# A top-k attention kernel: sums ahead of scores, the output copy behind the exponentials, key sums on GpSimd

## The reference

```python
q, k, v = split((xn @ Wqkv.T + bqkv))            # 16 heads of 8 channels, 256 rows
q, k = layernorm(q), layernorm(k)                # over the 8 channels
aw = softmax(q @ k.T / sqrt(8))                  # 256 x 256 for each head
aws = aw * (aw >= 12th largest of the row)       # top 5%
o_s = (aws / (sum(aws) + 1e-8)) @ v
qf, kf = softmax(q), softmax(k)                  # over the 8 channels
o_l = (qf @ (kf.T @ v)) / (qf . sum_rows(kf) + 1e-6)
o = sigmoid(alpha) * o_s + (1 - sigmoid(alpha)) * o_l
y = x + o @ Wproj.T + bproj + (xn @ W[idx] + b[idx])
```

## Time and profile before

| | before |
|---|---|
| median of three runs | 1290.69 us (1289.84 to 1293.82) |
| profiled execution | 1291.26 us, span of its instructions 1289.5 us |
| PE busy | 985.1 us, 76% |
| DVE busy | 1203.7 us, 93% |
| ACT busy | 1099.0 us, 85% |
| POOL busy | 1024.9 us, 79% |

### The profile page before, as it was taken

How to read it: one execution, slowest core, us unless ns; L and a number is a source line. 1 busy time by engine, 2 the same in 40 slices (tenths; PEclk the granted TensorE clock), 3 DMA queues, 4 the chain that set the end, 5 groups by cost and what they waited for, 6 DMA issues and landing times.

```text
span 1289.5 us, 38488 instructions
## 1 busy us (share of the span) xinstructions
PE 985.1 (76%) x9028; PEld 663.3 (51%) x9028; DVE 1203.7 (93%) x4585; ACT 1099.0 (85%) x3658; POOL 1024.9 (79%) x1560
## 2 busy tenths in 40 slices
PE   2578878888787777787877787777778788878876
PEld 0355555555455554555545555555545555555554
DVE  7699999999899998989989999999999999999994
ACT  2598989989899888979979989889988889989885
POOL 4587888988788887878968888888887888888864
PEclk9999999989899998989989999899999999999999
DMA  2122221212221222221222221222221222221120
GB/s 59 45 71 75 79 77 45 63 55 80 81 80 37 69 60 77 79 68 46 68 60 79 79 75 39 57 71 80 79 80 33 63 67 79 79 79 52 48 59 14
DMA packets 165203, 83.36 MB, mean 65 GB/s; under 512 B 7753, under 2 KB 164943, under 8 KB 164946
## 3 DMA queue, kind: packets, MB, share of 16 engines
q1 hardware_dynamic: 164946, 80.56, 21.7%
HBM read 42.78 MB, written 37.75 MB: 62 GB/s over the span
## 4 chain that ended last, share of the span: by engine, by line
DVE 31%; issue 24%; PE 18%; ACT 15%; POOL 6%; DVEq 4%; DMA 1%; SPq 0%; ACTq 0%; POOLq 0%
DVE rest L531 12%; DVE top L524 11%; ACT e L720 9%; DVE next L537 4%; POOL below L389 4%; PE turn_ps L831 4%; DVEq L73 3%; PE pv_ps L863 2%; ACT kept L685 2%; PE pv_ps L905 2%; PE turn_ps L832 2%; PE pv_ps L902 2%; PE work_ps L948 1%; ACT part L754 1%; PE score_ps L814 1%
## 5 line engine op out<-in xcount | busy, mean ns | idle before, releaser
L389 POOL TENSOR_SCALAR below<-e,next 128x256 bf16<-128x256 f32 x768 | 698.1, 928 | 0.0
L720 ACT ACTIVATE e<-score_ps,drop 128x256 f32<-128x256 f32 x1024 | 475.4, 490 | 68.1 <-POOL drop L367 67.2
L831 PE MATMUL turn_ps<-ident,e 128*128 128x128 f32 x2048 | 411.7, 294 | 28.1 <-issue 20.3
L531 DVE MATCH_REPLACE8 rest<-e 128x256 f32<-128x256 f32 x1024 | 413.8, 407 | 0.3
L537 DVE MAX8 next<-rest 128x8 f32<-128x256 f32 x1024 | 410.6, 411 | 0.8
L832 PE MATMUL turn_ps<-minus_huge,below 128*128 128x128 bf16 x2048 | 390.0, 228 | 0.0
L524 DVE MAX8 top<-score_ps 128x8 f32<-128x256 f32 x1024 | 360.0, 413 | 26.7 <-issue 15.0
L831 PEld LDWEIGHTS turn_ps<-ident,e 128*128 128x128 f32 x2048 | 303.8, 148 | 85.7 <-issue 42.5
L685 ACT ACTIVATE kept<-turn_ps 128x1024 f32<-128x1024 f32 x256 | 270.1, 1055 | 41.1 <-PE turn_ps L832 40.5
L720 ACT ACTIVATION_READ_ACCUMULATOR e<-score_ps,drop 128x1 f32 x1024 | 226.2, 221 | 0.0
L832 PEld LDWEIGHTS turn_ps<-minus_huge,below 128*128 128x128 bf16 x2048 | 225.7, 110 | 0.3 <-issue 0.2
(11 more groups left out here) (154 smaller groups left out, 1345.5 us busy)
## 6 DMA issues: line engine op xcount, KB each, us to landing
part_slots<-part SPq DMA_DIRECT2D x128, 192.0 KB, 2.3
q_slots<-part_slots SPq DMA_DIRECT2D x64, 256.0 KB, 3.5
k_slots<-part_slots SPq DMA_DIRECT2D x64, 256.0 KB, 4.1
part_slots<-part SPq DMA_DIRECT2D x64, 128.0 KB, 1.9
x_sb<-in_L_attn_x SPq DMA_DIRECT2D x32, 128.0 KB, 3.8
x_res<-in_L_attn_x SPq DMA_DIRECT2D x32, 128.0 KB, 4.0
out_y<-out_sb SPq DMA_DIRECT2D x32, 128.0 KB, 4.2
w_ops<-in_L_ffn_W SPq DMA_DIRECT2D x1, 512.0 KB
```

The source lines that it names most:

```text
L389: nc.gpsimd.tensor_scalar(below[:, r, t, :], e[:, r, t, :], next8[:, r, t, TOPK - 9:TOPK - 8], None, ALU.is_lt).then_inc(s["below_pool"], 1)
L531: nc.vector.match_replace(rest[:, t, :], e8[:, (u_ - 1) % 2, t, :], e[:, (u_ - 1) % RING, t, :], REMOVED).then_inc(s["rest_ready"], 1)
L720: nc.scalar.activation(e[:, u_ % RING, t, :], score_ps[:, u_ % 2, t // 2, t % 2, :], ACT.Exp, bias=drop[:, u_ % 2, t, 0:1], accum_out=z[:, ...
L831: mm(dst, e[:, r, t, keys], ident[:], start=True, stop=False, is_transpose=True)
```

## The change

Three edits:

1. On TensorE `sums()` of the sixth unit is called ahead of `early` and the scores, no longer behind the scores.
2. On GpSimd three additions (8 columns to 4 to 2 to 1, on 32 groups) make `k_sum` behind the comparisons of the sixth unit; VectorE's reduction goes. The reciprocal and the product stay, and wait for the same semaphore as before.
3. On ScalarE the copy to `out_sb` in the fourth unit stands behind that unit's exponentials and comparison, no longer ahead of them.

```diff
@@ tensors and semaphores
+        k_half = sb("k_half", [P, NT * H, 4])
+        k_quarter = sb("k_quarter", [P, NT * H, 2])
-            dmax_ready dsub_ready dexp_ready ksum_ready krec_ready feat_ready
+            dmax_ready dsub_ready dexp_ready ksum_step ksum_ready krec_ready feat_ready
@@ GpSimd
+                    if u_ == 5 and exists(it + 1):
+
+                        pool.wait_ge(s["dexp_ready"], 2 * (it + 2))
+                        src = k_exp[:].rearrange("p t (h d) -> p (t h) d", d=D)
+                        for i, (dst, w) in enumerate(((k_half[:], 4), (k_quarter[:], 2),
+                                                      (k_sum[:].unsqueeze(2), 1))):
+                            if i:
+                                pool.wait_ge(s["ksum_step"], 2 * (it + 1) + i)
+                            nc.gpsimd.tensor_tensor(dst, src[:, :, 0:w], src[:, :, w:2 * w], ALU.add).then_inc(
+                                s["ksum_step" if i < 2 else "ksum_ready"], 1)
+                            src = dst
@@ VectorE
-                    if u_ == 5 and exists(it + 1):
-                        if k == 5:
-
-                            dve.wait_ge(s["dexp_ready"], 2 * (it + 2))
-                            nc.vector.tensor_reduce(k_sum[:], k_exp[:].rearrange("p t (h d) -> p (t h) d", d=D), AX_X,
-                                                    ALU.add).then_inc(s["ksum_ready"], 1)
@@ ScalarE, ahead of the exponentials
-                    if u_ == 3 and exists(it - 2):
-                        act.wait_ge(s["w_out"], it - 1)
-                        wait(act, s["y_stored"], 16 * (it - 2))
-                        nc.scalar.copy(out_sb[:], pv_ps[:, 0:NT * C].rearrange("p (t c) -> p t c", t=NT)).then_inc(
-                            s["y_ready"], 1)
@@ ScalarE, behind the exponentials of keys and queries
+                    if u_ == 3 and exists(it - 2):
+                        act.wait_ge(s["w_out"], it - 1)
+                        wait(act, s["y_stored"], 16 * (it - 2))
+                        nc.scalar.copy(out_sb[:], pv_ps[:, 0:NT * C].rearrange("p (t c) -> p t c", t=NT)).then_inc(
+                            s["y_ready"], 1)
@@ TensorE
+                    if u_ == 5 and exists(it - 1):
+                        sums()
                     early(u_)
                     if exists(it if u_ < UNITS - 1 else it + 1):
                         scores(u_)
-                    if u_ == 5 and exists(it - 1):
-                        sums()
                     late(u_)
```

## The result

| | before | after |
|---|---|---|
| median, runs taken together on one chip | 1290.26 us (1289.61 to 1293.82) | 1255.66 us (1254.20 to 1259.08) |
| profiled execution, span | 1291.26, 1289.5 us | 1259.08, 1257.4 us |
| granted clock, mean | 0.958 | 0.967 |

The ratio is 0.973, 95% interval 0.9703 to 0.9757: 34.6 us less by the medians. The profiled execution of the kernel after is the slowest of its four, and its span is 32.1 us shorter than that of before; what follows explains these 32.1 us.

A forecast was written before the change was run, and what follows sets the result against it. VectorE, 93% busy, plus one wait per batch was taken as the bound. Gains of 28.0 + 9.9 us, less 2 and 3, took the profiled 1291.26 to 1258.4, so 1258 us; range 1251 to 1267, eight in ten 1250 to 1273.

The forecast's parts named there:

- VectorE's path is its work plus one wait: A normal batch, 37.75 us, is VectorE's work plus its 0.91 us wait for the sums' transposes; savings shorten the run.
- Term of the sums: Sixth unit, TensorE: transposes ahead of the scores remove VectorE's wait in 30 batches, 28.0 us gained.
- Term of the tree: VectorE loses the key sums' reduction, 0.32 us between starts, 31 times: 9.9 us gained.
- GpSimd's additions: Behind the sixth unit's thresholds, three additions take 1.1 us, covered by 1.47 us of idle time left on GpSimd.
- VectorE held by GpSimd: VectorE's replacements come 0.06 us later beside each tree of additions on GpSimd, 31 times: 2 us lost.
- The output copy: Fourth unit, ScalarE: the copy behind the exponentials frees 1.4 us that is slack, not gain: 0 us.
- Jumps and half clock: Behind the five loop jumps VectorE waits for TensorE at half clock, so part of the gain is lost: 3 us.
- rival 1: The earlier VectorE meets other late work in a batch's first units, giving back 16 us: 1274 us, chance 0.12.
- The rival of TensorE's clock: Half-clock stretches come into most batches, 3 us each; with 21 such batches 1321 us, chance 0.06.
- The wait stays: The sums' transposes still wait for ScalarE's later copy of oT, so VectorE waits as before: 1283 us, chance 0.05.
- VectorE stands still: VectorE stands for the whole 1.1 us of GpSimd's additions, 34 us in all: 1290 us, chance 0.03.

The follow-up runs named there:

- 1 + 3: Kernel before with the sums ahead of the scores and the output copy moved, VectorE's reduction kept: 1265.67 us, ratio 0.9798.
- 1: Kernel before with only the sums' transposes moved ahead of the remainder matmul and the scores: 1268.44 us, ratio 0.9832.
- 1 + 2: Kernel before with the sums ahead and the key sums added on GpSimd, output copy in its old place: 1262.02 us, ratio 0.9774.

## Why the prediction was right, and where it was not

The forecast was 1258 us, and 1255.66 came. The mechanism was right for the two terms that make the gain; that the number is so near is in part luck, as the sum below shows.

- *VectorE's path is its work plus one wait*: shown for the normal batch, which fell from 37.76 to 36.34 us, and by each of the first two edits by itself about as worked out. The prediction's list of waits left out a third, 11.3 us for scores in 10 places, and it is one of those that grew.
- *Term of the sums, 28.0 us*: per batch 0.99 us had been counted, 1.09 came. What was missed is that the step behind the wait is slower in the loop: 0.22 us from the denominators to the next maxima when VectorE had waited, 0.10 when not.
- *Term of the tree, 9.9 us, by the spacing of starts*: right in size in normal batches (0.32 to 0.36 us) and between "1 + 3" and the whole (10 us), but 6.4 us between "1" and "1 + 2" and 0.4 alone. The prediction added the terms without asking what each is worth alone. Why the other batches give it back without the sums is only in part shown, by the longer batches at the jumps.
- *GpSimd's additions, 1.1 us in a reserve of 1.47*: 1.14 us measured; 0.27 us of waiting is left, 0.37 by the forecast.
- *VectorE held by GpSimd, -2 us*: wrong, no run shows any. The 0.13 us of the earlier trace rows was read as a hold by the tree. Such a step occurs in 6 of 1024 pairs of the profile before, all six beside a squares' tree, but at one place of the loop, once in each of its six rounds; 24 other loads stand beside the same tree with the ordinary 0.06 us. The three other kernels that keep VectorE's reduction have six as well, the ten without it none, though all have the squares' tree, and the doubled tree has none beside it. So the odd step goes with the place in VectorE's code; what makes it is open. The rule of the Trainium skill (page "Perfetto Trace Analysis", section "Optimizing Scalar/DVE Operations"), that moving work between the two may not help since they share a port, did not decide here: for these instructions, with one tensor read each on VectorE's side, no run shows a hold.
- *The output copy, 0 us*: the size was off. It is worth 3 us alone, 3 with the sums (1268.44 - 1265.67) and about 6 with both others, the last just short of clear, and none of it in normal batches of the changed kernel. Why it matters is open; one profile of each is little, and written out the effect can't be told from nothing.
- *Jumps and half clock, -3 us*: mis-sized. The extra over normal batches grew by 8.5 us. Of that 6.2 are in the five batches with a jump: they got 0.18 us shorter each, where the other 24 got 1.33 us shorter. The prediction let some 0.5 us of the gain through there, and it counted only the waits for scores; the standing at the jump itself grew too, from 15.0 to 17.8 us in all. The other 2.3 us are mostly small waits for scores in batches without a jump: a part of rival 1 came true within the forecast.

The sum by what was measured: 29 batches of 1.42 us are 41.2 us, less 8.5 us of extra, is 32.7, and the profiled spans differ by 32.1. The forecast had 37.9, less 2 and 3. What it missed on the side of the gain (3.3 us, and 2 for a hold that isn't there) and on the side of the loss (5.5 us) cancelled: that is luck. The rival of TensorE's clock did not come: its mean rose from 0.958 to 0.967. "The wait stays" and "VectorE stands still" are refuted by the profile after.

## What to carry to other kernels

When one engine goes through a batch without a pause but for one wait, take its batch from one instruction to its next occurrence: work, by the distance between starts, plus that wait plus the slower step behind it. Ask of each edit what it is worth alone and behind the others: the same 0.3 us of every normal batch were worth 0.4, 6 and 10 us. Compare the normal batch and the rest apart: here the first followed the arithmetic to 0.1 us, while the second, with jumps back and half clock, held 29.8 us, and writing the loop out of the changed kernel was worth three quarters of the whole change.

## What the runs showed of the hardware

- A jump back of a loop of four batches leaves VectorE standing for 2.7 to 4.7 us (2.7 to 3.5 before, 3.1 to 3.7 after, 3.9 to 4.7 with smaller first loads), and TensorE's granted clock is 0.50, which is 1.2 of 2.4 GHz, in the stretch behind (483.6 to 493.8 us above). Five jumps and what followed cost 25.5 us (1255.66 - 1230.12).
- Behind a wait the step from the denominators to the next maxima is 0.22 us in the loop and 0.12 in the written-out batches, and 0.10 us without a wait. ScalarE's wait ahead of the output copy is 1.12 us in the loop and 0.93 written out. For the step the trace shows a register instruction in between that only the loop has.
- A reduction of 256 columns that is recorded with 401 ns costs 0.32 to 0.36 us a batch.
- GpSimd's three small additions beside VectorE's removals and maxima cost VectorE nothing that the profiles show.
